# Decoder layer and cross attention: ScalarE's order, VectorE's share of the turned probabilities, and the value biases

## The reference, cut to what matters

```
def mha(q_in, kv_in, wq, bq, wk, bk, wv, bv, wo, bo, mask, causal):
    q, k, v = q_in @ wq + bq, kv_in @ wk + bk, kv_in @ wv + bv      # (B, 64, 16 * 64)
    scores = q k^T per head;  masked keys (and later keys, if causal) = -inf
    attn = nan_to_num(softmax(scores / 8));  return (attn @ v) @ wo + bo

x = layer_norm(mha(x, x, ..., causal=True) + x)        # layer 0
x = layer_norm(mha(x, ctx, ..., causal=False) + x)     # layer 1
x = layer_norm(relu(x @ w1 + b1) @ w2 + b2 + x)        # feed-forward
q, k = rope(x @ Wq) / 8, rope(ctx @ Wk)                # layer 2, no biases
x = layer_norm(x + softmax(q k^T, masked) @ (ctx @ Wv) @ Wo)
```

## Time and profile before

| | us |
|---|---|
| median of three runs | 562.89 (562.7 to 564.36) |
| profiled execution | 563.51 |
| its span | 561.6 |
| PE busy | 519.6 (93%) |
| PEld busy | 472.7 (84%) |
| DVE busy | 447.3 (80%) |
| ACT busy | 341.1 (61%) |
| POOL busy | 299.5 (53%) |

### The profile page before, as it was taken

How to read it: one execution, slowest core, us unless ns; L and a number is a source line. 1 busy time by engine, 2 the same in 40 slices (tenths; PEclk the granted TensorE clock), 3 DMA queues, 4 the chain that set the end, 5 groups by cost and what they waited for, 6 DMA issues and landing times.

```text
span 561.6 us, 23619 instructions
## 1 busy us (share of the span) xinstructions
PE 519.6 (93%) x10336; PEld 472.7 (84%) x10336; DVE 447.3 (80%) x796; ACT 341.1 (61%) x873; POOL 299.5 (53%) x572
## 2 busy tenths in 40 slices
PE   6879999999999999999999999888899999999995
PEld 6668989989898898898888988778888888898885
DVE  4788777676787777777877777889898999999983
ACT  6447657575777767656557575556454566567462
POOL 2533434543635444333625336868666777777744
PEclk9879999999999999999999999989999999999999
DMA  8900000000011110000000000000000000000000
GB/s 237 318 25 4 2 2 2 2 3 3 4 39 41 40 40 3 2 3 1 4 2 2 2 2 4 1 2 3 4 8 8 7 13 8 8 13 8 7 14 15
DMA packets 10837, 12.73 MB, mean 23 GB/s; under 512 B 752, under 2 KB 8432, under 8 KB 10736
## 3 DMA queue, kind: packets, MB, share of 16 engines
q1 hardware_dynamic: 10736, 11.24, 6.7%
HBM read 10.18 MB, written 1.05 MB: 20 GB/s over the span
## 4 chain that ended last, share of the span: by engine, by line
PE 70%; DVE 15%; POOL 5%; ACT 5%; issue 3%; DMA 1%; SPq 0%; POOLq 0%; ACTq 0%; DVEq 0%
PE ps_p L595 13%; PE ps_p L439 9%; PE ps_p L440 7%; PE ps_p L441 7%; PE ps_p L567 6%; PE ps_a L493 5%; PE ps_a L514 5%; POOL kT L1022 4%; DVE turn L804 4%; PE ps_a L475 3%; PE ps_p L559 3%; PE ps_p L620 3%; PE ps_p L561 3%; PE ps_p L560 3%; DVE probs L916 2%
## 5 line engine op out<-in xcount | busy, mean ns | idle before, releaser
L1040 POOL TENSOR_TENSOR small<-mv,epsilon 128x1 f32<-128x1 f32 x48 | 18.1, 377 | 179.5 <-DVE mv L843 179.5
L595 PE MATMUL ps_p<-wo,headsT 128*128 128x128 f32 x768 | 93.8, 275 | 1.9 <-ACT headsT L664 1.3
L595 PEld LDWEIGHTS ps_p<-wo,headsT 128*128 128x128 f32 x768 | 90.5, 192 | 3.8 <-ACT headsT L664 1.4
L804 DVE TENSOR_TENSOR turn<-ps_p,rope 128x1024 f32<-128x1024 f32 x64 | 76.4, 1220 | 7.3 <-PE ps_p L441 3.9
L674 ACT ACTIVATE probsT<-ps_p 128x512 f32<-128x512 f32 x96 | 52.9, 612 | 45.1 <-PE ps_p L567 45.0
L901 DVE TENSOR_REDUCE total<-probs 128x16 f32<-128x1024 f32 x48 | 58.1, 1210 | 25.7 <-ACT probs L718 23.4
L692 ACT ACTIVATE headsT<-ps_a 128x512 f32<-128x512 f32 x60 | 32.6, 595 | 67.6 <-PE ps_a L514 67.6
L708 ACT ACTIVATE probs<-ps_a,top 128x64 f32<-128x64 f32 x256 | 56.3, 357 | 17.8 <-DVE top L872 15.9
L439 PE MATMUL ps_p<-xT_hi,wq_hi 128*128 128x256 f32 x192 | 60.4, 315 | 6.3 <-DVE xT_lo L791 3.5
L567 PE MATMUL ps_p<-eye,probs 128*128 128x128 f32 x384 | 54.0, 278 | 4.2 <-DVE probs L916 2.8
L672 ACT ACTIVATE vv<-ps_p 128x512 f32<-128x512 f32 x96 | 57.4, 625 | 0.1
(11 more groups left out here) (139 smaller groups left out, 1390.0 us busy)
## 6 DMA issues: line engine op xcount, KB each, us to landing
out<-y_out SPq DMA_DIRECT2D x16, 64.0 KB, 1.9
X<-in_x SPq DMA_DIRECT2D x1, 768.0 KB, 8.1
across<-in_across SPq DMA_DIRECT2D x1, 704.0 KB, 10.2
wq_raw<-in_L_xattn_sa_wq SPq DMA_DIRECT2D x2, 256.0 KB, 3.1
wk_raw<-in_L_xattn_sa_wk SPq DMA_DIRECT2D x1, 512.0 KB, 5.1
wv_raw<-in_L_xattn_sa_wv SPq DMA_DIRECT2D x1, 512.0 KB, 8.0
wo<-in_L_xattn_sa_wo SPq DMA_DIRECT2D x1, 512.0 KB, 9.0
wo<-in_L_xattn_ca_wo SPq DMA_DIRECT2D x1, 512.0 KB, 9.4
```

Of the source, the lines that this page charges most:

```text
L595: last = mm(bank[:, 0:E], headsT[:, p, :, :].rearrange("r b q -> r (b q)"), wo[:, layer % 2, p, :], start=(p == 0), stop=(p == PAIRS - 1))
L804: ins = V.tensor_tensor(turn[:, j % 2, :, :].rearrange("d a (h b t) -> d a h b t", h=2, t=S), bank[:, None, :].broadcast_to([128, 2, 512]) ...
```

## The change

- Turned probabilities (P): in the steps that aren't by head both tiles are copied out of the ring by VectorE, except in the last steps (u of 46 and on), where ScalarE takes the first and VectorE the second.
- Projections: ScalarE empties tiles 0, 1 and 2 and VectorE tile 3 (before: VectorE tile 1).
- Feed-forward steps of the second layer: the turned input FT comes first; ScalarE empties both F1 tiles, which stand together.
- ScalarE's order in those steps (`scalar_order`): input and values first, then both exponentials, then `heads_out`, then the projections.
- VectorE's order: maxima, input's low part, subtractions, turned tiles, sum, first multiply, one more, second multiply, weights.
- By-head steps: the second half of the multiply by the reciprocal is done by ScalarE, a step later, in eight instructions of one head each (`normalise_rest`), behind the values; VectorE's next reciprocal waits for it.
- Value biases: TensorE multiplies bv, broadcast, with wo in eight accumulating products a layer, in step 1 ahead of P; ScalarE reads the result. GpSimd's `before_1`, its memset of ones and two semaphores go.
- Masks: `masks` in step 2, the causal part in step 3, `keys_at_all` in four parts in steps 4 to 7, all ahead of the wait for the exponentials; the first one ahead of step 0.

```diff
+def turned_by(u):
+    return "AA" if by_head(u) else "AD" if u >= N - 2 else "DD"
-    probabilities = [("P", j, "A") for j in range(2)] if turns(u) and not defers(u) else []
+    probabilities = [("P", j, turned_by(u)[j]) for j in range(2)] if turns(u) and not defers(u) else []
-            project.append((name + "r", j, "D") if rotary(u) else (name, j, "ADAA"[j]))
+            project.append((name + "r", j, "D") if rotary(u) else (name, j, "AAAD"[j]))
     if ffn_chunk(u) is not None:
-        k = len(project) // 2
-        return heads + early[:1] + [("FT", 0, "AD")] + early[1:] + probabilities + project[:2] + [("F1", 0, "A")] \
-            + project[2:k] + [("F1", 1, "D")] + project[k:] + [("F2", 0, "D")] + result + late + next_in
+        return [("FT", 0, "AD")] + early + probabilities + project[:2] + [("F1", 0, "A"), ("F1", 1, "A")] + project[2:] \
+            + [("F2", 0, "D")] + result + late + next_in
...
-    before = [("norm", u - 1, 0), ("norm", u - 1, 1)] if by_head(u - 1) else []
+    before = [("norm", u - 1, 0)] if by_head(u - 1) else []
...
-    head = [("max", 0)] + ([] if split_heads(u) else [("max", 1)]) + before + [("shift", 0), ("shift", 1)]
-    n = 1 if u % 2 == 0 and projected(u) is not None or ffn_chunk(u) is not None else 0
-    return head + emptied[:n] + [("sum", 0)] + emptied[n:n + 1] + [("weights", 0), ("norm", u, 0)] + emptied[n + 1:n + 2] \
-        + [("norm", u, 1)] + emptied[n + 2:] + ffn_out
+    names = [fills(u)[at][0] for _, at in emptied]
+    turn_in = [e for e, n in zip(emptied, names) if n == "FT" or n == "T" and u % 2 == 0]
+    turned = [e for e, n in zip(emptied, names) if n == "P"]
+    rest = [e for e in emptied if e not in turn_in + turned]
+    early, late = ([("weights", 0)], []) if u == UNITS else ([], [("weights", 0)])
+    return [("max", 0)] + ([] if split_heads(u) else [("max", 1)]) + before + turn_in + [("shift", 0), ("shift", 1)] + turned \
+        + early + [("sum", 0), ("norm", u, 0)] + rest[:1] + [("norm", u, 1)] + late + rest[1:] + ffn_out
+
+def scalar_order(u):
+    emptied = [(at, n, j) for at, (n, j, who) in enumerate(fills(u)) if "A" in who]
+    late_values = u > 0 and u % UNITS == 0
+    ahead = [e for e in emptied if e[1] in ("PP", "O", "FT") or e[1] == "T" and u % 2 == 0 or e[1] == "V" and not late_values]
+    return ahead, [e for e in emptied if e not in ahead]
...
             def bias_of_values():
-                pe.wait_ge(bv_folded, 2)
+                pe.wait_ge(first_loaded, 16)
+                pe.wait_ge(wo_loaded, 32)
                 for layer in range(2):
-                    last = mm(ps_a[:, 2 + layer, 0:E], ones, turn[:, layer, :, :].rearrange("r h d -> r (h d)")[:, 0:E],
-                              start=True, stop=True)
+                    for p in range(PAIRS):
+                        last = mm(ps_a[:, 2 + layer, 0:E], bv[:, layer, p:p + 1].broadcast_to([128, 128]), wo[:, layer, p, :],
+                                  start=(p == 0), stop=(p == PAIRS - 1))
                     last.then_inc(bvwo_done, 1)
...
+            def normalise_rest(u):
+                act.wait_ge(dve_step, VSTEP.at(u, "recip" if split_heads(u) else "rinv"))
+                factor = inv if split_heads(u) else rinv
+                for n in range(8, 16):
+                    ins = nc.scalar.activation(probs[:, u % 2, n, :], probs[:, u % 2, n, :], ACT.Copy, scale=factor[:, n:n + 1])
+                ins.then_inc(normed_rest, 1)
...
+                if by_head(u - 1) and not by_head(u):
+                    normalise_rest(u - 1)
...
                         empty(u, at, name, j)
+                        if by_head(u - 1) and (name, j) == ("V", 1):
+                            normalise_rest(u - 1)
                     continue
-                for at, (name, j, who) in enumerate(fills(u)):
-                    if "A" not in who:
-                        continue
-                    if waiting and name not in ("O", "T", "PP"):
-                        exponentials(u, waiting.pop(0))
+                ahead, behind = scalar_order(u)
+                for at, name, j in ahead:
                     empty(u, at, name, j)
...
+                if attends(u):
+                    for j in range(2):
+                        exponentials(u, j)
+                if finishes(u) and not heads_in_ring(u):
+                    heads_out(u)
+                if u == 1:
+                    for layer in range(2):
+                        act.wait_ge(bvwo_done, layer + 1)
+                        nc.scalar.activation(bvwo[:, layer, :], ps_a[:, 2 + layer, 0:E], ACT.Copy).then_inc(bvwo_read, 1)
+                for at, name, j in behind:
+                    empty(u, at, name, j)
...
+                elif name == "P":
+                    ins = V.tensor_copy(probsT[:, j, :], bank[:, :])
...
             def sums(u):
-                if u == 0:
-                    keys_at_all(0, slice(0, READY), FIRST_MASKED, FIRST_VALID)
+                beside_exponentials(u)
                 dve.wait_ge(exped, EXPED.at(u, 1))
                 V.tensor_reduce(total[:, :], probs[:, u % 2, :, :], AX_X, ALU.add).then_inc(dve_step, 1)
                 dve.wait_ge(dve_step, VSTEP.at(u, "sum"))
+                if by_head(u - 1):
+                    dve.wait_ge(normed_rest, NORMED_REST.at(u - 1))
                 V.reciprocal(inv[:, :], total[:, :]).then_inc(dve_step, 1)
...
+            def beside_exponentials(u):
+                if u == 2:
+                    masks(slice(READY, UNITS))
+                elif u == 3:
+                    causal_masks(slice(READY, UNITS), MASKED - 1)
+                elif u in VALID:
+                    kind, units, count = VALID[u]
+                    keys_at_all(kind, units, MASKED, count)
```

More of the change, by code:

```diff
@@ L324, in build @@
         normed = sem("normed")
+        normed_rest = sem("normed_rest")
         weighted = sem("weighted")
@@ L521, in weight_values, with out_of_bank @@
                     last.then_inc(weighted, 1)
+            def out_of_bank(u, name, j):
+                who = {(n, k): w for n, k, w in fills(u)}[name, j]
+                if "A" in who:
+                    pe.wait_ge(act_emptied, EMPTY_A.at(u, name, j))
+                if "D" in who:
+                    pe.wait_ge(dve_emptied, EMPTY_D.at(u, name, j))
             def bank_free(u, at):
@@ L766, in _ @@
                             act.wait_ge(first_loaded, 16)
-                for j in waiting:
-                    exponentials(u, j)
+                if attends(u):
+                    for j in range(2):
+                        exponentials(u, j)
+                if finishes(u) and not heads_in_ring(u):
+                    heads_out(u)
+                if u == 1:
[4 more added lines that the diff above has]
+                    empty(u, at, name, j)
         @block.vector
```

84 lines of the change are left out of this document (26 added, 58 removed).

## The result

| | before | after |
|---|---|---|
| median, us | 562.8 (562.45 to 564.36, 4 runs) | 558.64 (558.16 to 559.04, 4 runs) |
| span of the profiled execution, us | 561.6 | 557.3 |

The ratio is 0.9921, interval 0.99 to 0.9941: faster by 4.2 us, where 12.9 were forecast (550 from 562.89). It lies at the upper end of the range of 545 to 559.

The account below looks back on a forecast made before the run. TensorE was taken to bound the first two layers, VectorE's order the last. Terms -6.1 - 0.85 - 1.3 - 7.5 + 0.3 + 1.8 = -13.65 from 563.5 gave 549.9, forecast 550 us, range 545 to 559.

Parts of the forecast that it names:

- rival C: First two layers: VectorE becomes the bound if a turned copy costs 1.275 us; 18 us slower, 568 us; chance 0.08.
- step 2 from 32.1: Sign of being right: step 2's scores begin near 32.1 us in place of 37.91.
- Tail, +1.8: Steps 46 and 47: unit 45's scalings come first on ScalarE and delay the values product; 1.8 us remain by the end.
- Last layer, -7.5: Steps 36 to 45: ScalarE takes the multiply's second half, freeing VectorE; four pairs at -1.6 and -1.1 for steps 36 and 37.
- A pair becomes 9.65 + 10.45: Last layer: odd step 9.65 us plus even step 10.45 gives a pair of 20.1 in place of 21.74.
- Rival A: Last layer is held by the rotation loop, so -7.5 becomes about -1 and the time 556.5 us; chance 0.13.
- Steps 3 to 29, -2.15: First two layers: -1.3 us from ScalarE's order and turned copies on VectorE, -0.85 from moved key masks.
- rival B: Even steps: split, subtraction, exponential and heads chain 0.5 us longer through hand-overs; 14 steps cost 7 more, 557 us; chance 0.08.
- the -0.35: Nine plain odd steps: unhindered key projections shorten each by 0.35 us, -3.15 in all.
- the key masks' term: Key-mask work spread over steps 2 to 7: 2.7 us saved, less 0.8 and 1.0 in steps 5 and 7; -0.85.
- Steps 0 to 2, -6.1: Bias fold moved from GpSimd to TensorE: step 2's scores 5.8 us earlier, step 2 itself gains some 0.3.
- 16 products, 1.95: Step 1: the 16 bias products priced by the output projection's 16 products, 1.95 us with the pipeline's end, some 1.8 on the path.

Follow-up runs that it names:

- e6: Changed kernel with VectorE doing both multiply halves of unit 45, so step 46 has no ScalarE scalings: 557.02 us, ratio 0.9902.
- e13: Changed kernel with the tail (steps 46 to 48) ordered as before the change and unit 45 wholly on VectorE: 554.62 us, ratio 0.9862.
- e12: Changed kernel, five edits: even-step heads first, unit 45 on VectorE, bias products split, key tile early (1, 5, 7), scalings behind relu tiles (33, 35): 540.44 us.
- e14: The five edits of e12 on the changed kernel, with the tail ordered as before the change too: 540.84 us, ratio 0.961.
- e2: Changed kernel with ScalarE copying the heads ahead of both exponentials in all steps outside the rotary ones: 551.27 us, ratio 0.9792.
- e15: e12 with the first two layers' turned tiles copied by ScalarE again, behind exponentials and heads: 568.45 us, ratio 1.011 to the kernel before.
- e8: Changed kernel with VectorE multiplying only 8 columns of one head for units 36 to 43, a timing-only version: 557.78 us, ratio 0.9912.
- e5: Changed kernel with the heads copied ahead of the exponentials in even steps alone: 547.8 us, ratio 0.974.
- e9: Changed kernel with the second layer's eight bias products issued behind step 1's key tiles: 557.72 us, ratio 0.9903.
- e10: Changed kernel with VectorE taking its key tile ahead of the first probability multiply in steps 1, 5 and 7: 557.05 us, ratio 0.9894.
- e11: Changed kernel with ScalarE scaling twelve of sixteen heads of the rotary units and VectorE four: 562.71 us, ratio 1.0.

## Why the prediction was off

The sign, the place of the gains and the rejection of rival C (a turned copy at 1.275) were right; the sum was too large by 9.3 us. Of its own signs these came true: turned copies of 0.6 (0.64), odd steps shorter by 0.35 (0.30), even ones longer by 0.2 to 0.4 (0.3, and 0.54 in the second layer). These didn't: step 2 from 32.1 (33.41), a pair of the last layer at 20.1 (20.70), the values product of step 46 two us later (1.35). Four terms were mis-sized.

1. *Tail, +1.8, measured +5.0.* The scalings alone cost 3.0 in step 46 (11.93 against 8.90 in e6), and not by what was priced. The wait brings the values product to 4.77 us into the step, 1.35 later than before and not the two forecast. But then TensorE's products run at a lower clock, which the forecast put at nothing: the rest of the step takes 7.16 us where e6 has 5.41. In the stretch behind the wait, 527.57 to 531.49, and the next one, the mean granted clock was 0.69 and 0.85 of full speed; from 529.50 to 532.00 it was 0.50, the lower of the two levels:

```profile
527.57:531.49 3.92, 3.92 (x70) 3.13 (x71) 0.00 (x0) 1.68 (x3) 0.00 (x0) 0.69 0.06 18
531.49:534.73 3.24, 3.24 (x25) 3.12 (x23) 1.68 (x2) 2.12 (x4) 0.00 (x0) 0.85 0.01 3
...
529.50:532.00 2.50, 2.50 (x9) 1.93 (x8) 0.00 (x0) 1.40 (x4) 0.00 (x0) 0.50 0.02 7
```

With the wait at 0.78 (e6) it stayed at 1.00. I had priced the wait and not what follows it. Of the other 2.0, 1.4 are the "issue" stall and 0.5 the order of the tail (e6 and e13, e12 and e14). Before, a stall of 1.88 stood in step 34 instead, and that step's 12.18 us are 10.98 after: more than the whole -1.0 of steps 30 to 35. So the two places nearly cancel.

```profile
398.70 0.35 PE L475 MATMUL ps_a<-kT,qT 32*64 32x64 f32 x10 [1.88 <-issue]
```

A stall's length alone doesn't tell whether the clock falls. Behind this one it stayed at 1.00 (first row below, of the kernel before). Behind the stalls of 1.64 and 1.67 in step 47 of e2 and e15 it fell to 0.50 (second and third row), and step 47 took 24.26 and 24.22 us there in place of the changed kernel's 22.52:

```profile
398.70:402.00 3.30, 3.30 (x66) 3.10 (x70) 2.52 (x3) 2.33 (x9) 0.00 (x0) 1.00 0.00 0
531.50:534.50 3.00, 3.00 (x21) 2.30 (x14) 0.44 (x1) 1.68 (x3) 0.74 (x2) 0.50 0.10 27
550.00:552.50 2.50, 2.50 (x10) 2.03 (x9) 0.00 (x0) 1.73 (x4) 0.00 (x0) 0.50 0.10 26
```

2. *Last layer, -7.5, measured -4.4.* Steps 36 and 37 came as forecast (-1.0 for -1.1). "A pair becomes 9.65 + 10.45" was wrong in both parts: 10.68 and 10.02. VectorE did come free, as the step said (0.74 idle). But TensorE's own stream is 10.0 us in the even step and 10.3 in the odd one (10.68 less the wait of 0.35), so 9.65 was below what it can do; this is 1.8 us over three pairs. In odd steps the remaining half of the multiply also stands beside GpSimd's addition (without it the step is 0.42 shorter, the pair 0.33, e8). What VectorE lost by a multiply beside an addition was priced in the forecast; what GpSimd loses by it was not, though the addition of 1.72 in the earlier trace rows had that loss in it already. "SBUF - State Buffer" of the Trainium skill ("SBUF: two separate sides") says that the pair of ports shared by the two engines is an exclusive lock and the loser blocks. By that rule the second addition would lose, as an estimate, the 0.6 us in which the multiply overlaps it (478.78 to 479.37). The trace has 0.44 for the two additions (2.96 against 2.52), so it agrees in direction and not in size. Rival A (the rotation holds the layer) was thus right in kind, at about a quarter of its price: without the multiply steps 36 to 45 take 1.6 us less (e8), where A had 6.5. The last pair, steps 44 and 45, lost another 0.76 against its like, which no edit explains.

3. *Steps 3 to 29, -2.15, measured +0.7.* Mostly the even steps, in rival B's direction at about a quarter of its price: they cost 6.2 where the sum had 4.3, with 0.3 each in the first layer instead of 0.2, 0.54 in the second instead of 0.38 (step 14, which splits two inputs, belongs there, and the sum had it in the first), and 1.0 in step 16 instead of 0.8. Rival B's mechanism, late hand-overs, isn't what the trace shows. The chain that I followed (input, split, subtraction, exponentials, heads) was right in every link: the heads are done 6.69 us into step 12, where the sum had 6.74. The output projection then starts 6.84 into the step (6.79 forecast, 6.60 before), and the step still ends 0.32 later than before. Besides, the -0.35 was taken for steps 3, 5 and 7 too, where the wait for the key tile hides it: those three lost 0.85 together, the key masks' term alone, not 1.9. The other odd steps lost 0.30 each, the feed-forward steps 2.9 for 2.45. The larger point is one that the forecast stated and didn't weigh: the heads' place behind the exponentials was the whole of the even steps' loss (e2, e5), 0.7 to 1.0 a step against an order that the same engines allow.

4. *Steps 0 to 2, -6.1, measured -4.8.* "16 products, 1.95": the row says x16 for eight products, since a product of this kind is two records. Sixteen are x32 and 3.73 us. Step 1 began 0.66 earlier than forecast (21.79 for 22.45), took 11.62 for 9.65, and step 2 began 1.3 late. With eight products off the path (e9) the step is 10.37.

The key masks came as forecast: waits for kT of 0.94 and 1.21 in steps 5 and 7 for the forecast 0.8 and 1.0 (e10 takes most of them back). The scalings were 2.01 for eight in place of 1.8, inside the bounds. "VectorE: DVE Perf Modes" of the Trainium skill (the TRN2 errata) puts ScalarE's fixed cost from SBUF above that from PSUM: 0.04 us a piece, an estimate from its cycles. The trace agrees: the scalings start 0.24 apart back to back, the exponentials from PSUM of that size 0.20. The 0.22 of the forecast was busy time divided by the count, which has the last one's full length in it; and no run separates the source from the function, copy or exponential.

What stays open: what the stall "issue" is. It stood at the same record (the last 36 of a values product in step 47) in the changed kernel and in all fourteen made from it, at 0.8 to 1.7 us, but in step 34, or in steps 17 and 47, in the two with the old code. Steps 44 and 45 are longer than their like in most of those kernels as well, by up to 1.1 together, and in step 44 of the changed kernel a gap of 0.26 in a query tile is put down to "issue" too. It is also open why the clock fell behind some stalls and not behind others.

## What to carry to other kernels

When an engine's queue is reordered, write down for each copy who waits for it and when it could start: in step 12 the heads were ready at 136.2 and copied from 139.55, behind exponentials whose sum had slack in an even step (in an odd one it had not, e2). When an edit adds a wait on TensorE, give the products behind it a price at the lower clock as well: here the clock cost 1.7 us where the wait cost 1.3. Count a row's instructions against the code before its duration is used as a unit, and compare steps, not totals: two stalls of 1.5 us that the edit has no part in by the code hid most of a gain of 3.9.

## What the runs showed of the hardware

- TensorE idle for 2.08 and 2.25 us was followed by stretches at a mean of 0.69 and 0.59 of the full clock, with the lower of its two levels (1.2 and 2.4 GHz) in them; eight output products took 3.11 us in place of 1.95. After a wait of 0.78 in the same place (e6) the clock stayed at 1.00. After stalls of 1.64 and 1.67 in step 47 it fell to 0.50, after one of 1.88 in step 34 it stayed at 1.00.
- GpSimd's two additions of 128x512 took 2.52 us without VectorE's multiply beside them (e8), 2.69 beside the one over four heads (e11), and 2.96 beside the one over eight.
- Moving two copies of 128x512 a step from VectorE to ScalarE cost 28 us in all, though ScalarE is busy in only 63% of steps 2 to 29 there (201.5 us of 318.2): TensorE waits 0.88 us a step for the copy behind the exponentials and the heads. The kernel before has the same copies on ScalarE in another order, with odd steps of 9.64 in place of 10.48. So the copy's place in the queue counts here more than the engine's load.
